# Layer 0 attention: the difference map as fp16 high part and remainder, turned by DMA transposes instead of TensorE

## What is computed

```
A1 = einsum('bhqd,bhkd->bhqk', Q1, K1) * scaling
A2 = einsum('bhqd,bhkd->bhqk', Q2, K2) * scaling
attn = softmax(A1, axis=-1) - lam * softmax(A2, axis=-1)
O = einsum('bhqk,bhkd->bhqd', attn, V)
O = O / sqrt(mean(O*O, axis=-1) + EPS) * rms_scale * (1 - LAMBDA_INIT)
out = einsum('bne,de->bnd', heads of O side by side, Wo)
```

## Time and profile before

| | |
|---|---|
| median of 3 runs | 1832.75 us (1830.62 to 1835.07) |
| span of the profiled execution | 1821.8 us |
| median above that span | 10.95 us |
| PE busy | 1623.5 us (89%) |
| DVE busy | 1278.5 us (70%) |
| ACT busy | 1091.0 us (60%) |
| POOL busy | 1137.6 us (62%) |
| mean granted TensorE clock | 0.954 |
| first and last `combine` | 31.5 us and 803.1 us |

### The profile page before, as it was taken

How to read it: one execution, slowest core, us unless ns; L and a number is a source line. 1 busy time by engine, 2 the same in 40 slices (tenths; PEclk the granted TensorE clock), 3 DMA queues, 4 the chain that set the end, 5 groups by cost and what they waited for, 6 DMA issues and landing times. The chain is left out here.

```text
span 1821.8 us, 32230 instructions
## 1 busy us (share of the span) xinstructions
PE 1623.5 (89%) x12272; PEld 1362.4 (75%) x12272; DVE 1278.5 (70%) x2640; ACT 1091.0 (60%) x2250; POOL 1137.6 (62%) x1102
## 2 busy tenths in 40 slices
PE   5999999999999999999986788885599578998997
PEld 4888888888888888877775677774588456666675
DVE  7888888788887888754346177748853687777782
ACT  3677767766776667764545465553244356666665
POOL 4888899999999999995007465454466562223311
PEclk9999999999999999999997999996799889999999
DMA  3000000000100000000002510004145400000000
GB/s 96 12 4 1 16 1 15 1 15 1 39 1 1 1 1 1 1 24 6 1 9 80 172 28 3 2 2 124 32 119 142 101 11 1 2 2 1 2 2 24
DMA packets 64090, 50.08 MB, mean 27 GB/s; under 512 B 10673, under 2 KB 55761, under 8 KB 63809
## 3 DMA queue, kind: packets, MB, share of 16 engines
q1 hardware_dynamic: 53328, 34.40, 6.4%
q0 software_dynamic: 8496, 12.59, 3.2%
q10 hardware_dynamic: 2112, 1.05, 0.2%
HBM read 37.53 MB, written 10.49 MB: 26 GB/s over the span
## 5 line engine op out<-in xcount | busy, mean ns | idle before, releaser
L757 POOL TENSOR_TENSOR dtl<-dts,dth 128x512 fp32r<-128x512 f32 x256 | 353.7, 1382 | 20.5
L687 DVE TENSOR_REDUCE nm<-PS 128x1 f32<-128x1024 f32 x256 | 311.4, 1217 | 26.4 <-PE PS L207 25.4
L2102 ACT ACTIVATE ET_a<-PS 128x256 f32<-128x256 f32 (+2 forms) x512 | 219.9, 500 | 120.1 <-PE PS L1995 73.2
L755 POOL CAST dth<-dts 128x512 fp32r<-128x512 f32 x256 | 233.6, 913 | 52.5 <-ACT dts L614 51.4
L205 PE MATMUL PS<-xh,yh 128*128 128x512 f32 x512 | 224.9, 439 | 11.5 <-ACT XNT L607 5.3
L148 PE MATMUL PS<-C,XN 128*128 128x128 f32 x1120 | 175.1, 282 | 44.7 <-DVE XN L200 39.2
L207 PE MATMUL PS<-xh,yl 128*128 128x512 f32 x512 | 204.1, 399 | 0.0
L206 PE MATMUL PS<-xl,yh 128*128 128x512 f32 x512 | 203.9, 398 | 0.0
L607 ACT ACTIVATE XNT<-PS,nm 128x1024 f32<-128x1024 f32 x128 | 142.7, 1115 | 77.4 <-DVE nm L687 76.4
L614 ACT ACTIVATE dts<-PS 128x512 f32<-128x512 f32 x256 | 152.5, 598 | 49.0 <-POOL dtl L757 48.9
L148 PEld LDWEIGHTS PS<-C,XN 128*128 128x128 f32 x1120 | 138.8, 144 | 55.0 <-issue 39.2
(11 more groups left out here) (453 smaller groups left out, 4303.8 us busy)
## 6 DMA issues: line engine op xcount, KB each, us to landing
e_wg<-in_WgT SPq DMA_DIRECT2D x16, 256.0 KB, 2.7
e_wu<-in_WuT SPq DMA_DIRECT2D x16, 256.0 KB, 3.1
e_wd<-in_WdT SPq DMA_DIRECT2D x16, 256.0 KB, 3.8
m_x_rows<-m_xs SPq DMA_DIRECT2D x1, 1472.0 KB, 5.1
m_xs<-m_x_rows SPq DMA_DIRECT2D x5, 256.0 KB, 4.7
m_y_rows<-m_xs SPq DMA_DIRECT2D x5, 256.0 KB, 3.6
X<-in_L_attn_X SPq DMA_DIRECT2D x2, 512.0 KB, 5.1
wqn<-in_L_attn_Wq SPq DMA_DIRECT2D x8, 128.0 KB, 2.2
```

The costliest lines, as they stand in the source:

```text
L687: e.tensor_reduce(self.nm[:, half, i:i + 1], self.S[half], AX.X, MAX, negate=True).then_inc(*self.top.up((g, half)))
L755: e.tensor_copy(hi, src).then_inc(*ts.up((g, g4, "h")))
L757: e.tensor_tensor(lo, src, f(hi), SUB).then_inc(*ts.up((g, g4, "l")))
L2102: e.activation(dst, src, ACT.Exp, scale=self.SC, bias=0.0).then_inc(*self.ex.up(it))
```

## The change

D is no longer turned by TensorE. ACT copies D to fp16 (`take_high`, the high part `dh`), POOL subtracts that from D and writes the remainder as fp16 (`take_low`, `dl`), and SP issues two DMA transposes per tile, one of each part, from SBUF to SBUF (`dth`, `dtl`, now fp16 with three slots). To keep D within the range of fp16, the exponent of half 0 gets a shift per head (`shift`), added to the row maximum by one more DVE instruction (L695 of the changed kernel), and the tokens are scaled by 256 (`XUP`) before they are split to fp16; the scale is taken out again in `gather`. `meet` multiplies fp16 operands. The two PSUM banks of the transposes become a third score buffer, so that the six half maps of three tiles go round three buffers. D has three buffers instead of two, `dh` and `dl` four slots each. The pipeline is deeper: `meet` follows 6 iterations behind the scores (before: 4), `weigh`, `square` and `take_out` 9 (before: 7).

```diff
--- before.py
+++ after.py
@@ Attn0.__init__
-    TAIL = 7
+    TAIL = 9
+    UP = 16.0
+    XUP = 256.0
...
-        self.dth, self.dtl = sb("dth", [128, 2, 8, 256], F32R), sb("dtl", [128, 2, 8, 256], F32R)
-        self.xnh, self.xnl = sb("xnh", [128, NT, 128], F32R), sb("xnl", [128, NT, 128], F32R)
+        self.dh, self.dl = sb("dh", [128, 4, 1024], F16), sb("dl", [128, 4, 1024], F16)
+        self.dth, self.dtl = sb("dth", [128, 3, 8, 256], F16), sb("dtl", [128, 3, 8, 256], F16)
+        self.xnh, self.xnl = sb("xnh", [128, NT, 128], F16), sb("xnl", [128, NT, 128], F16)
...
-        self.S = [k.bank(0, 2), k.bank(2, 2)]
+        self.S3 = [k.bank(0, 2), k.bank(2, 2), k.bank(4, 2)]
@@ sp
-        for h in range(2, self.H):
-            q.wait_ge(self.job_pe, ("prep", h - 2))
-            q.wait_ge(self.w_split, ("vl", h - 2))
-            load(h)
+        for g in range(self.NG):
+            p, n = g // 2, slice(128 * (g % 2), 128 * (g % 2) + 128)
+            h = g // 16 + 2
+            if g % 16 == 3 and h < self.H:
+                q.wait_ge(self.job_pe, ("prep", h - 2))
+                q.wait_ge(self.w_split, ("vl", h - 2))
+                load(h)
+            if p >= 3:
+                q.wait_ge(self.met, (p - 3, 1))
+            for x, made, src, dst in (("h", self.d_high, self.dh, self.dth), ("l", self.d_low, self.dl, self.dtl)):
+                q.wait_ge(made, g)
+                e.dma_start_transpose(dst[:, p % 3, :, n], src[:, g % 4, :]).then_inc(*self.landed[g % 4].up((g, x)))
+
+    def S(self, g, half):
+        return self.S3[(2 * g + 1 - half) % 3]
@@ pe: scores, turn, meet, loop
-            if g:
-                q.wait_ge(self.exped, (g - 1, half))
+            if 2 * g + 1 - half >= 3:
+                n = 2 * g + 1 - half - 3
+                q.wait_ge(self.exped, (n // 2, 1 - n % 2))
...
-            for j in range(4):
-                n = 512 * g4 + 128 * j
-                t = self.k.tr(e, self.TB[g4][:, 128 * j:128 * j + 128], self.D[g % 2][:, n:n + 128])
-            t.then_inc(*self.turned.up((g, g4)))
...
-            q.wait_ge(self.t_split, (2 * p + 1, hf, "l"))
+            if hf == 0:
+                for g in (2 * p, 2 * p + 1):
+                    q.wait_ge(self.landed[g % 4], (g, "l"))
...
-            if 0 <= g - 4 < self.NG:
-                meet((g - 4) // 2, g % 2)
-            if mid:
-                turn(g - 2, 1)
+            if 0 <= g - 6 < self.NG:
+                meet((g - 6) // 2, g % 2)
@@ act
-        def turn(g, g4):
-            q.wait_ge(self.turned, (g, g4))
-            if g:
-                q.wait_ge(self.t_split, (g - 1, g4, "l"))
-            e.activation(self.dts[:, g4, :], self.TB[g4], ACT.Copy).then_inc(*self.copied.up((g, g4)))
+        def take_high(g):
+            q.wait_ge(self.combined, g)
+            if g >= 4:
+                q.wait_ge(self.landed[g % 4], (g - 4, "l"))
+            e.activation(self.dh[:, g % 4, :], self.D[g % 3], ACT.Copy).then_inc(*self.d_high.up(g))
...
-            if 0 <= g - 3 < self.NG:
-                turn(g - 3, 1)
-            if 0 <= g - 7 < self.NG:
-                square(g - 7)
             if 0 <= g - 2 < self.NG:
-                turn(g - 2, 0)
+                take_high(g - 2)
+            if 0 <= g - self.TAIL < self.NG:
+                square(g - self.TAIL)
@@ dve: top
+            e.tensor_reduce(self.nm[:, 0, i:i + 1], self.S(g, 0), AX.X, MAX, negate=True).then_inc(*self.top0.up(g))
+            h = g // 16
+            q.wait_ge(self.shift_set, "s")
+            q.wait_ge(self.top0, g)
+            e.tensor_tensor(self.nm[:, 0, i:i + 1], self.nm[:, 0, i:i + 1], self.shift[:, h:h + 1], ADD).then_inc(*self.top.up((g, 0)))
@@ combine
-        if g >= 2:
-            q.wait_ge(self.turned, (g - 2, 1))
+        if g >= 3:
+            q.wait_ge(self.d_low, g - 3)
...
-        e.scalar_tensor_tensor(out=self.D[g % 2], in0=self.E[g % 2][:, 1, :], scalar=self.ratios[:, i:i + 1],
+        e.scalar_tensor_tensor(out=self.D[g % 3], in0=self.E[g % 2][:, 1, :], scalar=self.ratios[:, i:i + 1],
@@ pool
-        def split(g, g4):
...
-            e.tensor_copy(hi, src).then_inc(*ts.up((g, g4, "h")))
-            q.wait_ge(ts, (g, g4, "h"))
-            e.tensor_tensor(lo, src, f(hi), SUB).then_inc(*ts.up((g, g4, "l")))
+        def take_low(g):
+            if g >= 4:
+                q.wait_ge(self.landed[g % 4], (g - 4, "l"))
+            q.wait_ge(self.d_high, g)
+            e.tensor_tensor(self.dl[:, g % 4, :], self.D[g % 3], self.dh[:, g % 4, :], SUB).then_inc(*self.d_low.up(g))
...
+            e.tensor_scalar(xs, k.XN[:, t, :], self.XUP, None, MUL).then_inc(*self.x_split.up((b, "s")))
+            q.wait_ge(self.x_split, (b, "s"))
+            e.tensor_copy(self.xnh[:, t, :], xs).then_inc(*self.x_split.up((b, "h")))
             q.wait_ge(self.x_split, (b, "h"))
-            e.tensor_tensor(self.xnl[:, t, :], k.XN[:, t, :], f(self.xnh[:, t, :]), SUB).then_inc(*self.x_split.up((b, "l")))
+            e.tensor_tensor(self.xnl[:, t, :], xs, self.xnh[:, t, :], SUB).then_inc(*self.x_split.up((b, "l")))
```

More of the change, by code:

```diff
@@ L406, in __init__ @@
         self.rms_t = k.sig("rms_scaled", ["r"])
-        self.x_split = k.sig("xn_split", grid(range(2), "hl"))
+        self.x_split = k.sig("xn_split", grid(range(2), "shl"))
         self.w_split = k.sig("w_split", [(n, h) for h in heads for n in ("o0", "o1", "vh", "vl")])
@@ L414, in __init__ @@
         self.recip, self.ratio, self.combined = k.sig("sum_recip", tiles), k.sig("ratio", tiles), k.sig("combined", tiles)
[L415 to L418, removed]
+        self.shift_set = k.sig("lam_shift", ["m", "s"])
+        self.top0 = k.sig("score_max_raw", tiles)
+        self.d_high, self.d_low = k.sig("d_high", tiles), k.sig("d_low", tiles)
+        self.landed = [k.sig(f"dt_landed{i}", grid(range(i, NG, 4), "hl"), 16) for i in range(4)]
         self.met = k.sig("tokens_met", grid(range(NG // 2), range(2)))
@@ L564, in pe @@
                 q.wait_ge(s.lam_exp, "e")
+                q.wait_ge(self.shift_set, "m")
                 s.turn(e, q, 3)
@@ L619, in gather @@
                 q.wait_ge(self.job_pe, ("uo", 2 * p - 3))
-            e.activation(self.zh[:, p % 2, :], self.ZB, ACT.Copy).then_inc(*self.z_high.up(p))
+            e.activation(self.zh[:, p % 2, :], self.ZB, ACT.Identity, scale=1.0 / self.XUP, bias=0.0).then_inc(*self.z_high.up(p))
         def square(g):
@@ L633, in act @@
                 exps(g - 1, 0)
-            if g % 2 == 0 and 0 <= g // 2 - 3 < self.NG // 2:
-                gather(g // 2 - 3)
-            if 0 <= g - 3 < self.NG:
-                turn(g - 3, 1)
-            if 0 <= g - 7 < self.NG:
-                square(g - 7)
+            if g % 2 == 0 and 0 <= g // 2 - 4 < self.NG // 2:
+                gather(g // 2 - 4)
             if 0 <= g - 2 < self.NG:
-                turn(g - 2, 0)
+                take_high(g - 2)
+            if 0 <= g - self.TAIL < self.NG:
+                square(g - self.TAIL)
             if g < self.NG:
@@ L707, in dve @@
                 share(g - 1)
-            if g % 2 == 0 and 0 <= g // 2 - 3 < self.NG // 2:
-                gather(g // 2 - 3)
+            if g % 2 == 0 and 0 <= g // 2 - 4 < self.NG // 2:
+                gather(g // 2 - 4)
             if g < self.NG:
                 top(g, 1)
-            if 0 <= g - 7 < self.NG:
-                take_out(g - 7)
+            if 0 <= g - self.TAIL < self.NG:
+                take_out(g - self.TAIL)
             if 0 <= g - 1 < self.NG:
@@ L888, in bank_free @@
         if x not in self.prev:
-            if b < 4:
-                q.wait_ge(a.exped, (a.NG - 1, b // 2))
-            elif b < 6:
-                q.wait_ge(a.copied, (a.NG - 1, b - 4))
+            if b < 6:
+                n = next(n for n in reversed(range(2 * a.NG)) if n % 3 == b // 2)
+                q.wait_ge(a.exped, (n // 2, 1 - n % 2))
             elif b == 6:
```

83 lines of the change are left out of this document (42 added, 41 removed).

## The result

The changed kernel takes **1969.27 us** (median of 4 runs, 1965.78 to 1972.76) against 1833.45 us before: a ratio of 1.0747, with a 95% interval of 1.0728 to 1.0766. Forecast were 1990 us, within 1870 to 2110. Its profiled execution took 1968.39 us, with a span of 1966.6 us.

The account below looks back on a forecast made before the run. TensorE was taken to bound the kernel before, with a DVE-ACT ring only 0.20 us a tile shorter. The lengthened ring, 7.31 against 6.08 us over about 125 tiles, plus 3 us, gave 1832.75 + 157 = 1990 us, range 1870 to 2110.

Parts of the forecast that it names:

- The held `combine`: On DVE, `combine` waits until 0.20 us before the end of POOL's subtraction, then ends 1.28 us later, at 4.43 us.
- The sum: Whole kernel: about 125 tiles x (7.31 - 6.08) = 154 us, and 3 for the loop's ends: 1832.75 + 157 = 1990 us.
- The ring: Layer 0's attention loop, ACT, POOL, DVE, ACT: 7.01 us odd tile, 7.28 even, mean 7.15, with the addition's holds 7.31.
- its holds: POOL's 1.90 and 2.39 us instructions hold DVE's new addition in two tiles of eight: 0.16 us a tile.
- PE's need: TensorE's work per tile without two groups of transposes, 0.72 us: falls from 6.08 to 5.36 us.
- Rival A: POOL's subtraction is shorter with fp16 operand and result; between 1.4 and 1.95 us gives 1870 to 1940 us; chance 0.12.
- Rival B: At the start of `combine` on DVE: it is not held, 5.62 us a tile, 1778 us; chance 0.13.
- Rival C: SP's queue of transposes bounds from 3.65 us each: 2076 us at 4 us, 2326 us at 5; chance 0.13.
- threshold of 3.65: On SP's queue: the time in us of one transpose from which two of them fill a tile of 7.31.
- The offset: Median of the runs shown stands 10.95 us above the profiled span of 1821.8 us; left standing, giving 1832.75.
- The clock: On PE: gaps in its work might lower the granted clock; at 1.2 GHz 5.36 us would be 10.7 a tile.

Follow-up runs that it names:

- e2: Changed kernel with ACT's copy of D moved behind the exponential of half 1: 2009.49 us, 1.0977 of the kernel before.
- e6: Changed kernel with POOL's subtraction in two instructions of 512 columns each: 1897.33 us, 1.0408 of the kernel before.
- e4: Changed kernel without POOL's subtraction, the second transpose turning the high part again: 1848.93 us, 1.0103 of the kernel before.
- e3: Changed kernel with the copy behind the exponential of half 1 and the addition's shift as scalar operand: 1809.54 us, 0.9887 of the kernel before.
- e9: e3 with DVE taking the maximum of half 1 ahead of the ratio: 1741.49 us, 0.9554 of the kernel before.
- e5: Changed kernel with one DMA transpose per tile, products reading the high part twice: 1955.10 us, 1.0728 of the kernel before.
- e7: e3 with two more DMA transposes per tile that nobody reads: 1939.80 us, 1.0650 of the kernel before.

## Why the prediction was right

**The held `combine`: right, and shown.** Its medians are 2.60 and 2.75 us, the ends fit POOL's to 0.01 us, and the hold moves with POOL's instruction (e2), shortens with its length (e6) and goes with it (e4). e3, in which the subtraction holds neither `combine` nor the addition, is the proof in time.

**The sum: one term too large.** The ring was put at 7.28 us for a tile with `zh`; it takes 7.15. The term that was mis-sized is the subtraction: 2.14 us, where I took 2.35 from the fp32 one. That is 0.21 us a tile, 26 us in all. POOL starts 0.15 us after the copy's end (505.55 to 505.70), where I had 0.06, and that gives 11 us back, so the two errors partly cancel. For a tile without `zh` the measured ring is shorter than forecast by the same 0.13 us:

```profile
511.29 0.19 ACT L610 ACTIVATION_READ_ACCUMULATOR XNT<-PS,nm 128x1 f32 x1
...
518.17 0.19 ACT L610 ACTIVATION_READ_ACCUMULATOR G<-PS,nm 128x1 f32 x1
```

From 511.48 to 518.36 it is 6.88 us against 7.01. The copy was 1.05 us (forecast 1.04), the addition 0.16 (0.18), and its holds come to 0.304 - 0.160 = 0.14 us a tile (0.16):

```profile
L695 DVE TENSOR_TENSOR nm<-nm,shift 128x1 f32<-128x1 f32 x112 | 34.1, 304 | 3.9
```

(busy us, mean ns of one, idle before; 100 to 900 us). So 7.13 us stand where 7.31 were forecast, and 125 x 0.18 = 22 us is the miss of 21 us.

**PE's need: near, as far as it can be read.** 5.36 us was forecast by taking two groups of transposes away; e9 comes to 5.42 with PE busy 96% of it, 5.2 us. What the prediction could not read, the rate of the fp16 products, makes little: they follow each other at 0.11 us, the twelve of 507.58 to 509.01 us in the kernel before at 0.12.

**Rival A, a shorter subtraction,** was true in direction: the subtraction with an fp16 operand and result takes 9% less, not the 17% or more (1.95 us or less) that the rival needed. **Rival B, `combine` not held,** is refuted. Its price of 5.62 us a tile has no run of its own; e3, in which the subtraction holds nothing, comes nearest and has 5.86. **Rival C, the transposes bound,** is refuted by e5. One lands in 3.1 us, within the forecast's 0.9 to 4.7 and below the threshold of 3.65; but the threshold took them one after the other, and they overlap: in e7 four that land in 3.2 us each go into a tile of 6.78. What counts is the 1.4 us of the DMA engines and 1.23 us of SP's queue:

```profile
505.63 1.23 SPq L454 DMA_TRANSPOSE dth<-dh  x1
```

By the Trainium skill, "VectorE: DVE Perf Modes", section "The three transpose paths", a transpose of eight blocks would take eight times 1309 ns, an estimate of 10.5 us; measured were 3.1 us to landing, so the measurement decides against going by that figure here. The Trainium skill's "Advanced Engine Details and Errata", section "X-Bar Transpose (TRN2)", puts such a DMA on a level with a plain one. The landings agree: plain 256 KB copies landed in 4.7 us and, `e_wg` of a later layer, in 2.7. The time of the DMA engines does not: a transpose took 1.4 to 1.5 us of them, where 0.9 was worked out for plain traffic of its size.

**The offset** between median and span that I let stand was not there: the changed kernel's profiled run is within 1 us of its median. Outside the loop the two profiled executions differ by another 10.6 us (144.8 us between the spans, 134.2 in the loop), which the medians don't show. Chips differ by as much: e5's loop takes 905.7 us, as the changed kernel's, yet its span is 14.6 us shorter, and on its chip the kernel before runs 11.7 us faster. On which chip the first profile was taken isn't recorded, so this cause is not shown.

**The clock** that I had named as a way to be wrong did fall. PE was busy 81% of the stretch instead of the 73% forecast: some 5.2 us of work in 7.13, at a mean clock of 0.91, would give 80%. It cost little, as PE mostly waits anyway: in 800 us DVE waits 12.9 us for PE. The changed kernel's PE had been idle 5.48 us until 506.45:

```profile
506.45 0.79 PE L205 MATMUL PS<-xh,mh 128*128 128x512 f32 x1 [5.48 <-DVE us L707]
507.90 0.44 PE L205 MATMUL PS<-dth,xnh 128*128 128x256 f16 x1
508.13 0.42 PE L206 MATMUL PS<-dtl,xnh 128*128 128x256 f16 x1
...
514.65 0.27 PE L206 MATMUL PS<-dtl,xnh 128*128 128x256 f16 x1
514.76 0.27 PE L207 MATMUL PS<-dth,xnl 128*128 128x256 f16 x1
```

Behind the gap the products follow each other at 0.21 to 0.23 us (the granted clock from 507 to 511 us is 0.56 on average, mostly 1.2 GHz); some 7 us on, at 2.4 GHz, at 0.11. At 512.09 DVE waits 0.30 us for these late scores, but the `combine` behind it ends at 515.80, which POOL's end at 514.72 gives: here the slow stretch cost nothing.

## What to carry to other kernels

Before work is moved off a full engine, write out the ring of the engines behind it: here it had 0.2 us of room, and the change put one long GpSimd instruction on it. Where GpSimd and VectorE both work in SBUF, ask of each VectorE instruction with two SBUF tensors, the smallest too, whether a wide GpSimd instruction is under way when it comes; move that instruction behind it, cut it, or give VectorE a scalar operand instead, and do so at every place at once, since removing one alone can make it slower (e2). A change that seems bad can hold a good one: with two small edits and another order the same idea is 4.5% faster than the kernel before.

## What the hardware showed beyond that

- The hold does not depend on the size of the held instruction: an addition on one element per partition took a median of 1.92 us in e2 instead of 0.16. With its second operand as a scalar per partition it takes 0.21 us in each of 128 cases, also in e3, where the subtraction is under way.
- A DMA transpose of 128x1024 fp16 within SBUF takes 3.1 us to land, 1.4 to 1.5 us of the 16 engines and 1.23 us of the issuing queue. Queue q1 had 323664 - 53328 = 270336 packets more for 67.1 MB, some 250 bytes each.
- A weight load of 128 columns takes 98 ns in fp16 beside 188 for one of the type that the profile calls f32 (means of e9, 100 to 900 us, at a mean clock of 0.98):

```profile
L207 PEld LDWEIGHTS PS<-xh,yl 128*128 128x128 f32 x452 | 84.8, 188 | 20.6
L205 PEld LDWEIGHTS PS<-dth,xnh 128*128 128x128 f16 x480 | 47.1, 98 | 48.9 <-issue 44.5
```
